# Turning the latent of an attention chunk: f32 products with two stacked identities, or plain transposes and a sum on VectorE

## What is computed

```python
kv_latent = x @ W_to_kv.T            # 512 -> 128
c = kv_latent @ W_compress.T         # 128 -> 64
mu = jnp.mean(c, axis=-1, keepdims=True)
var = jnp.mean((c - mu) ** 2, axis=-1, keepdims=True)
ch = (c - mu) * jax.lax.rsqrt(var + LN_EPS) * ln_gamma + ln_beta
q = ch @ W_q_comp.T
kv = ch @ W_kv_comp.T                # k and v; then rope, causal softmax, output projection
...
hidden = fwht(silu(x @ W1.T) * (x @ W3.T))   # feed-forward, 512 -> 2048
out = hidden @ W2.T
```

## Time and profile before

| what | value |
|---|---|
| median of 3 runs | 2259.26 us |
| the 3 runs | 2259.07, 2259.26, 2261.85 us |
| the profiled execution: its own time | 2261.15 us |
| its span, first to last instruction | 2259.4 us |
| TensorE busy | 2150.8 us, 95% |
| VectorE busy | 1443.1 us, 64% |
| ScalarE busy | 983.7 us, 44% |
| mean granted TensorE clock | 0.982 of full |

### The profile page before, as it was taken

One profiled execution on the slowest core, in us unless ns is written; L12 is line 12 of the kernel. 1 busy time (PEld: TensorE's weight loads), 2 busy tenths in 40 slices (PEclk: granted clock), 3 DMA queues, 4 the chain that ended last, 5 costly groups with the idle time before them and its releaser, 6 DMA issues. The chain is left out here.

```text
span 2259.4 us, 27494 instructions
## 1 busy us (share of the span) xinstructions
PE 2150.8 (95%) x10172; PEld 1020.9 (45%) x10172; DVE 1443.1 (64%) x2742; ACT 983.7 (44%) x1493; POOL 234.2 (10%) x212
## 2 busy tenths in 40 slices
PE   6778899999999999999999999999999999999999
PEld 3433444444444444444444444444444444444444
DVE  7876676766657675666757676576756666563333
ACT  6845454434444534434344344435344344442221
POOL 2344554000000000000000000000000000000000
PEclk8789999999999999999999999999999999999999
DMA  8344324332323333234233332333232342323221
GB/s 329 138 146 155 122 93 130 121 116 95 91 87 129 115 105 98 79 121 141 74 102 121 112 99 90 101 116 119 101 98 93 110 139 74 98 88 112 84 84 54
DMA packets 127654, 252.97 MB, mean 112 GB/s; under 512 B 74528, under 2 KB 74656, under 8 KB 122144
## 3 DMA queue, kind: packets, MB, share of 16 engines
q1 hardware_dynamic: 127520, 251.21, 33.5%
HBM read 194.81 MB, written 39.85 MB: 104 GB/s over the span
## 5 line engine op out<-in xcount | busy, mean ns | idle before, releaser
L767 PE MATMUL PF<-XF,WS 128*128 128x512 f16 x1792 | 685.2, 382 | 18.1 <-ACT PF L1124 10.3
L768 PE MATMUL PF<-XF,WS 128*128 128x512 f16 x1792 | 683.6, 381 | 0.0
L769 PE MATMUL PF<-XF,WS 128*128 128x512 f16 x1792 | 682.9, 381 | 0.0
L791 PE MATMUL PD<-W2S,H 128*128 128x512 f16 x1024 | 388.2, 379 | 0.0
L792 PE MATMUL PD<-W2S,H 128*128 128x512 f16 x1024 | 388.1, 379 | 0.0
L793 PE MATMUL PD<-W2S,H 128*128 128x512 f16 x1024 | 388.1, 379 | 0.0
L1135 ACT ACTIVATE SH<-PF,afs 128x512 f32<-128x512 f32 x256 | 176.0, 688 | 380.2 <-PE PF L769 379.4
L767 PEld LDWEIGHTS PF<-XF,WS 128*128 128x128 f16 x1792 | 176.6, 99 | 246.3 <-issue 38.3
L1731 DVE SCALAR_TENSOR_TENSOR SH<-PF,afs,SH 128x512 f32<-128x512 f32 x256 | 191.8, 749 | 141.0 <-ACT SH L1135 118.6
L1143 ACT ACTIVATE H<-SH 128x1024 f16<-128x1024 f32 x128 | 135.4, 1058 | 324.2 <-DVE SH L1731 324.2
L769 PEld LDWEIGHTS PF<-XF,WS 128*128 128x128 f16 x1792 | 176.2, 98 | 214.0 <-issue 4.4
(11 more groups left out here) (307 smaller groups left out, 2207.3 us busy)
## 6 DMA issues: line engine op xcount, KB each, us to landing
WS<-wscr SPq DMA_DIRECT2D x112, 896.0 KB, 4.6
W2S<-w2scr SPq DMA_DIRECT2D x30, 1024.0 KB, 4.9
xraw<-xT SPq DMA_DIRECT2D x58, 256.0 KB, 3.6
ring<-x SPq DMA_DIRECT2D x56, 256.0 KB, 4.3
wscr<-WS SPq DMA_DIRECT2D x16, 896.0 KB, 3.8
out<-ring SPq DMA_DIRECT2D x56, 256.0 KB, 2.4
XF<-w SPq DMA_DIRECT2D x16, 512.0 KB, 8.8
RAW<-w13t SPq DMA_DIRECT2D x16, 512.0 KB, 4.3
```

Source lines behind the costliest of these rows:

```text
L767: pe.matmul(bank, wh, th, start=i < 2 and j == 0, stop=False, skip_group_check=True)
L768: pe.matmul(bank, wh, tl, start=False, stop=False, skip_group_check=True)
L769: m = pe.matmul(bank, wl, th, start=False, stop=j == 1, skip_group_check=True)
L791: pe.matmul(PD[:, t % 2, :], th, wh, start=j == 0, stop=False)
```

## The change

The four f32 products by the stacked identities become four f32 transposes of full 128 x 128 blocks by the plain identity `idn`. Their result takes the whole bank of 512 columns: for each tile 64 columns of the high part and 64 of the low part. `lat(a, i)` names part `i` of it. ScalarE's `latent2` copies part 0 (256 numbers per partition, as before). A new VectorE step, `latent_sum(a)`, waits for `a_c0`, reads part 1 from the bank, adds the copy of part 0, writes the sum over the copy, and raises the new semaphore `v_c0`. What waited for `a_c0` (`squares`, `proj`, and `yfree` for the bank) now waits for `v_c0`. `latent_sum` stands at slot 6 in the loop and ahead of `squares` in the prologue.

```diff
+        def lat(a, i):
+            return banks(a)[1].rearrange("p (t c) -> p t c", t=4)[:, :, 64 * i:64 * i + 64]
...
             def latent(a):
                 for t in range(4):
-                    m = pe.matmul(b[:, t * 64:t * 64 + 64], xTc[:, t * 128:(t + 1) * 128], idd, start=True, stop=True)
+                    m = pe.transpose(b[:, t * 128:(t + 1) * 128], xTc[:, t * 128:(t + 1) * 128], idn)
                 m.then_inc(p_ct, 1)
-                yfree = (a_c0, one(a))
+                yfree = (v_c0, one(a))
...
             def proj(a):
-                w.wait_ge(a_c0, one(a))
+                w.wait_ge(v_c0, one(a))
...
             def latent2(a):
-                ac.activation(work(a)[0], banks(a)[1][:, 0:256], ACT.Copy).then_inc(a_c0, 1)
+                ac.activation(work(a)[0].rearrange("p (t c) -> p t c", t=4), lat(a, 0), ACT.Copy).then_inc(a_c0, 1)
...
+            def latent_sum(a):
+                c3 = work(a)[0].rearrange("p (t c) -> p t c", t=4)
+                w.wait_ge(a_c0, one(a))
+                ve.tensor_tensor(c3, lat(a, 1), c3, ALU.add).then_inc(v_c0, 1)
+
             def squares(a):
                 c0b, c1b, _ = work(a)
-                w.wait_ge(a_c0, one(a))
+                w.wait_ge(v_c0, one(a))
...
             def attention(a, slot):          # VectorE
                 if slot < 4:
                     conv(a, slot)
+                if slot == 6:
+                    latent_sum(a)
                 if slot == 7:
                     kept["squares"] = squares(a)
...
             ve.tensor_tensor(bb[:, :], U, wsm[:, BIAS:BIAS + 512], ALU.add).then_inc(v_bb, 1)
+            latent_sum(0)
             kept["squares"] = squares(0)
...
+            latent_sum(1)
             kept["squares"] = squares(1)
```

More of the change, by code:

```diff
@@ L321, in build_kernel @@
         v_cc, v_xl, v_wc, v_wf, v_pb, v_wg, v_wp = (sem(f"v_{s}") for s in ("cc", "xl", "wc", "wf", "pb", "wg", "wpl"))
+        v_c0 = sem("v_c0")
         v_V, v_rk, v_yk, v_rq, v_xq, v_K, v_Q = (sem(f"v_{s}") for s in ("V", "rk", "yk", "rq", "xq", "K", "Q"))
```

## The result

The changed kernel takes 2252.62 us (median of 7, 2251.15 to 2254.16) beside 2259.92 us for the kernel before (2259.07 to 2263.97). The ratio is 0.9964, with a 95% interval of 0.9953 to 0.9976: 7.3 us faster, where 5.05 were forecast. The direction was forecast right, but the gain is larger than the sum says. The time itself is still inside the range given (2252.3 to 2257.4). But that range was reckoned from a time of before of 2259.26 us, so that it allows a gain of 1.9 to 7.0 us, and 7.3 is more. So there are 2 to 3 us to find.

A forecast was written before the change was run, and what follows sets the result against it. TensorE's matmul stream was taken to bound the loop, VectorE the prologue. -5.6 (loop) + 0.45 + 0.1 (prologue) = -5.05 us from 2259.26 gave 2254.2, forecast as 2254.3, range 2252.3 to 2257.4.

The forecast's parts named there:

- TensorE's saving of 0.40 us per latent: Loop chunks 2 to 15: four transposes occupy 0.44 us where the products took 0.84; 5.6 us saved in all.
- The sum of 0.43 us on VectorE: Loop: hidden in a 2.02 us hole at odd chunks (margin 0.53) and idle time at even ones (0.75 left).
- the end of the cover: Loop: the sum is free within 0.53 us at odd chunks; uncovered, it costs 0.43 us at each even chunk.
- +0.45 and +0.1: Prologue: VectorE's sum adds 0.45 us at chunk 1, and 0.1 (0 to 0.45) at chunk 0, where it is mostly swallowed.
- the 0.8 us of chunks 2 and 3: First super-chunk: TensorE's saving there, 0 to 0.8 us for both chunks, was kept at 0.8, though less sure.
- Rivals 1 and 3: 1: gain returns as waiting, 2257.0 or 2260.2, chance 0.12; 3: transposes lower the loop's clock, 2284 in all, chance 0.03.
- Rival 2: Odd loop chunks: TensorE waits for v_c0 if the sum is stretched; 3.3 us back, 2257.5; chance 0.03.
- -5.6 + 0.45 + 0.1 = -5.05 us: Whole kernel: loop saving on TensorE plus the prologue's VectorE sums at chunks 1 and 0.
- comes off the end: Loop: TensorE's matmul stream sets the time, so anything removed shortens the kernel unless another engine makes it wait.
- -0.8 and +0.55: Forecast terms: TensorE's saving at chunks 2 and 3, and the prologue's added VectorE sums.
- The split of the times of before: Whole kernel: four executions before lay near 2259.1 or 2261.5 us, an unknown of some 2 us in the forecast.

The follow-up runs named there:

- e9: Changed kernel with the latent's four plain transposes made as f32 products with the 128-column identity: 2261.75 us, ratio 1.0004.
- e7: Changed kernel with three more VectorE sums ahead of the latent's sum in chunks 2 to 15: 2267.59 us, ratio 1.0028.
- e8: Changed kernel with the latent's four transposes made three times over in chunks 2 to 15, twelve in all: 2278.24 us, ratio 1.0073.
- e11: Changed kernel with 24 more already-met wait instructions on TensorE's queue while it waits for its first input: 2252.39 us, ratio 0.9966.
- e10: Kernel before with 24 more already-met wait instructions on TensorE's queue while it waits for its first input: 2269.27 us, ratio 1.0039.
- e5: Kernel before with 64 more already-met wait instructions on TensorE's queue at the program's start: 2274.28 us, ratio 1.0055.

## Why the prediction was right in direction and short in size

The steps, one by one. TensorE's saving of 0.40 us per latent: right at the 12 from chunk 4 on, and 0.45 at chunks 2 and 3; its cause is the transposing pass (e9). The Trainium skill, "TensorE: Matmul & The Clock Gate", part 4, has 275 ns for a transpose; the recorded durations agree (272 to 273 ns), and the starts say that it isn't what one occupies: 0.44 us for four, 1.31 for twelve. The sum of 0.43 us on VectorE, in a hole at odd chunks and in idle time at even ones: right (0.42; margins 0.65 and 0.72), and e7 found the end of the cover where it was forecast. The prologue: +0.45 and +0.1 were forecast; scores at chunk 1 start 0.33 us later. The loop starts at 115.70, 115.71 and 116.76 us with the new prologue (115.76 and 115.82 in e7 and e8) and at 116.09, 115.31 and 115.11 with the old: some 0.5 us later on average, a difference within their spread. Whether the 0.8 us of chunks 2 and 3 reach the end isn't shown either: group 0 differs by over 2 us between executions of one kernel. Rivals 1 and 3 fell: no wait took the gain back, and the clock stayed at 1.00 (e8), so that the rule of the same part, that transposes don't bring the full clock, is not seen here between streams of products; no run here has transposes alone in the loop for longer than 1.4 us. Rival 2's wait exists, and the sum has to end 0.65 us later for it to appear.

The step that failed is the sum itself, "-5.6 + 0.45 + 0.1 = -5.05 us": it takes for granted that whatever comes out of the stream of matmuls "comes off the end" and nothing else in the loop moves, and is set against a time of before that held 3.2 us of something else. The trace of before showed it: a wait of 2.2 us among its likes of 0.65, followed by half-clock matmuls. I had read one typical odd chunk and one typical even one and taken the loop for regular. With the missing term the sum is -5.05 - 3.2 = -8.25 us, beside -7.3 and -7.6 in the medians (and -8.5 in e11). Over the two profiles of each kernel the spans fall by 8.6 us on average: 6 x 0.86 in groups 1 to 6, 3.2 for the long wait, and some 0.3 for the smaller stretches; the start of the loop and group 0 together give nothing, where the sum has -0.8 and +0.55. The part of the change that brings the 3.2 us is one that I had not priced, 8 instructions fewer on TensorE's queue for each latent. That the fetch then missed all six places was luck, and nothing in the prediction foresaw it. The split of the times of before that I noted (2259.1 and 2261.5) isn't it, since both profiles of that kernel have the long wait.

What is shown: the long wait goes and comes with instructions that do nothing but take room in TensorE's queue, and it is there exactly when the fetch's packet falls into the transfer. What is only argued: that q8 is TensorE's instruction queue, from its packets' size and count and from their moving with the added instructions, and why a packet of 16 KB (0.9 to 1.6 us on its DMA engine) lengthens a transposing DMA from 2.4 to about 4 us. And open is what puts the fetch where it is: it isn't one instruction for one, as e10 showed.

No version beats the changed kernel for certain. The one with the change in the loop alone has the lowest median, 2250.97 beside 2252.56 in the same set, with executions that overlap (2249.56 to 2252.23 and 2250.59 to 2254.57); it leaves out the 0.55 us of the prologue, and its fetches miss all six places too (one falls on the second place, in group 5).

## What to carry to other kernels

When a kernel repeats a pattern, compare every repetition before summing: one that is 1 or 3 us longer than its likes is a term of the time of before, and any edit may remove or multiply it. A change in the number of instructions on an engine moves its instruction fetches against the transfers; with a gain of a few us, test it against a version that differs only in such a shift. For a transposition in f32 on TensorE, count the distance between starts: 0.11 us for a plain transpose of 128 x 128, 0.21 to 0.22 for a product by the identity, whether it has 64 columns or 128.

## What the runs showed of the hardware

- A 16 KB packet of the queue that I take for TensorE's instruction fetch, falling into a transposing DMA of 128 x 384 f16 in 16 of 78 places, lengthened it from 2.4 us to 3.7 to 4.4 us, and cost 1.3 to 3.7 us where TensorE waited for it closely. At the second place, where TensorE doesn't wait otherwise, the transfers took 4.1 and 3.6 us for 2.4 and 2.5, and TensorE waited 0.75 us and fell back by 0.9 (1317 us in the changed kernel; 0.5 to 1.2 us in 9 cases). A plain transfer of 256 KB took 4.9 us for 3.2.
- Wait instructions that are already met cost TensorE 0.108 us each (64 of them 6.9 us, e5).
- The granted clock fell to 0.50 for about 3 us behind 13 of the 16 long waits (about 2 us idle), and not behind the waits of 0.65.
- Transposes repeated for 1.3 us without a product between them left the granted clock at 1.00 (e8, 12 latents of the loop).
